# The second FFN product of an eight-batch transformer kernel, from float32 to a three-term split

## The chip, the cores and the metric

One core of one Trainium2 chip. The time is that of the device, in microseconds, of the whole program; the kernel before ran three times, the median counts.

## What is computed

An input x of 8 batches by 512 tokens by 256 features goes through a transformer of two layers, a test-time-training block, and the same transformer again:

```python
x = x + 0.5 * ffn_ref(_layernorm(x), ...)      # two layers of _layer, below
x = x + attn_ref(_layernorm(x), ...)           # TTT block, the "mid" stage
x = x + 0.5 * ffn_ref(_layernorm(x), ...)
# _layer: shift, h @ wqkv, l2norm, rotary, local attention (window 128), @ wo, residual, and then
h = layernorm(shift_token(x)) * lg + lb
a, g = split(h @ w1 + b1)                      # 256 -> 2 x 682
x = x + (a * gelu(g)) @ w2 + b2                # 682 -> 256: the product that is changed
```

The hidden width 682 is five tiles of 128 rows and a rest of 42 (`MT` = 6 tiles, `REST` = 42).

## The kernel before

Layers are numbered L = 0 to 3 (two passes of two), batches b = 0 to 7; each batch has four tiles t of 128 tokens. For each (L, b) every engine runs its own function `sequence`: four **tile stages** t = 0 to 3 (attention) and then an **FFN stage** of twelve jobs, six for each half of the batch (256 tokens). The order of the work is written out by hand, engine by engine; semaphores (`wait_ge`, `then_inc`) are the only coupling.

- **TensorE, a tile stage** (`sequence`, from line 1158): `S` (scores, in two halves, L1023), `A1` (the q, k and v products of the next tile, L963 to L965 with wqkv), `PT` (transposed probabilities, L1039), `PV` (L1053), `A0`, `A2` (transposes of k and q of the next tile, L999), `WO` (L963 to L965 with wo). At t = 2 comes `H2T` (transposed LayerNorm output of the first half). Between these stand pieces of `W2(prev, ...)`, the second FFN product of the batch **before**, cut by `cuts` into up to four fills: 12 instructions for each tile (each of the six matmuls of uT, 128 tokens, by w2, 256 columns, in float32 is recorded as two instructions at L1153).
- **TensorE, the FFN stage**: `W1` jobs 0 to 5, with `H2T` of the second half after the fifth, and jobs 6 to 11. These are 132 instructions, already split products: `split_product` (L963, L964, L965) makes upper by upper, upper by lower, lower by upper, in F32R.
- **VectorE, a tile stage**: `S` (a fused scale, mask and row minimum from PSUM, L1483), `R` (reciprocals), `A1` (eight operations of 512 columns for k and q of the next tile, L1450 to L1460, that use t1, t2 and write kqr), `O`, `A0`, `A2`, `WO` (the residual), `halves`, and `W2` (adds the second product, L1560). At t = 2 also the LayerNorm of the first half.
- **VectorE, the FFN stage**: `U` (L1553) makes uT = (a + b1) * gelu in one operation, straight from PSUM to the operand of `W2`. After the second job `LN_moments`, after the third `LN_apply` (L1544), after the fifth `H2T` (L1510).
- **ScalarE**: eight exponentials a tile stage (L733), then squares and PSUM copies; in the FFN stage twelve `G` (Gelu, L793 and L796), `H2T` after the fifth, and at the end `table(ACT.Exp)` (L783).
- **GpSimd**: `NP` (normalises the probabilities, L589), `A1` (powers and the scaling of kqr), `XB` (residual and b2 for `W2`, L596); in the FFN stage only the LayerNorm power (`LN`, L606), after which it takes the first `XB` of the next batch.

In the batches (0,0) and (2,0) there is no batch before, so their tile stages run with no `W2` at all.

Of the kernel before, what the change touches and what calls it, by code (L numbers as in the profile page):

```python
# [32 lines left out]
F32 = mybir.dt.float32  # L33
# [26 lines left out]
JOBS = (MT - 1, *range(MT - 1))  # L60


def build(nc, A):
    ctx = ExitStack()
    with ctx:
# [29 lines left out]
        w2 = sb("w2", [P, MT, D])  # L95
# [42 lines left out]
        gg = sb("gg", [P, 2, 2 * P])  # L138
        uT = sb("uT", [P, 2, MT, 2 * P])
# [5 lines left out]
        wo_s = nc.dram_tensor("wo_split", (DEPTH, P, HL * PAIRS * D), F32).ap()  # L145
        w1_s = nc.dram_tensor("w1_split", (DEPTH, P, KT * HL * W1W), F32).ap()
# [41 lines left out]
        u_done = sem("u_done", 3)  # L188
        w2_ps = sem("w2_ps", 4)
# [65 lines left out]
        m_up = [[cut(flat(sq[:, :, :], 512 * i + 256 * par, 256), NT) for par in range(2)] for i in pair]  # L255
# [32 lines left out]
        t_g, t_qd, t_a, t_m = (msems(k) for k in ("masked", "quadrant", "a_masked", "level_masked"))  # L288
        t_p_ps, t_p, t_i_ps, t_i, t_q = (msems(k) for k in ("mx_ps", "mx", "inverse_ps", "inverse", "inverse_quadrant"))
# [3 lines left out]
        s_zero = msem("hT_zero_again")  # L293
# [10 lines left out]
        def raw_piece(i):  # L304

            name, j = PIECES[i]
            if name == "wqkv":
                return cut(flat(uT[:, :, :, :], i * 1024, 1024), KT)
            if name == "wo":
                return cut(flat(w2[:, :, :], 0, PAIRS * D), PAIRS)  # L310
            return cut(flat((h, h2)[j][:, :, :], 0, 1024), KT)

        def raw_w1(j, k):
            lo, hi = W1_COLS[j]
            if j == 2:
                return flat((w2[:, 4:6, :], gg[:, :, :])[k], 0, hi - lo)
# [53 lines left out]
        def _(e):  # L370
# [27 lines left out]
            def load_rest(L):  # L398
# [58 lines left out]
            def load_out(b):  # L457
# [40 lines left out]
            def sequence(L, b, last=False):  # L498
# [50 lines left out]
            load_x(1)  # L549
# [1405 lines left out]
```

## Time and profile before

| | |
|---|---|
| median of 3 runs | 2788.74 us (2784.41 to 2792.33) |
| profiled execution | 2787.39 us, its span 2785.6 us |
| granted TensorE clock, mean | 0.995 |
| share of the span busy: PE, DVE, ACT, POOL | 98%, 75%, 59%, 48% |
| busy on L1153 (second FFN product), 1536 instructions | 435.8 us |
| chain that ended last: PE, DVE, issue, ACT | 77%, 10%, 6%, 6% |

Matmuls are pipelined, so the duration of one is longer than its distance to the next. What one costs is read from the distance between starts, in the timeline; a busy share of 98% says that something was in flight, not that the engine could take no more.

### The profile page before, as it was taken

How to read it: one execution, taken by the hardware profiler on the slowest of the kernel's cores; microseconds unless marked ns; L12 is line 12 of the kernel's file. 1: busy time of each engine (PE TensorE's matmuls, PEld its weight loads, DVE VectorE, ACT ScalarE, POOL GpSimd, SP SyncE). 2: the span in 40 equal slices, each digit the busy share in tenths (PEclk: the TensorE clock that was granted, in tenths of full speed). 3: DMA queues.
4: the chain of work that ended last, by engine and by line, in shares of the span. 5: the costliest groups of instructions: out<-in, count | busy, mean ns of one | idle time of the engine just before them, and what ended most of it. 6: DMA issues, size and time to landing. Idle time of an engine off the chain costs nothing.

```text
span 2785.6 us, 64354 instructions
## 1 busy us (share of the span) xinstructions
PE 2717.4 (98%) x22640; PEld 2316.1 (83%) x22640; DVE 2097.5 (75%) x6328; ACT 1633.0 (59%) x4358; POOL 1335.2 (48%) x1436
## 2 busy tenths in 40 slices
PE   7999999999999999998998999999999999999998
PEld 6788888888888888887766788888888888888887
DVE  7888888877777877776655778777777778777775
ACT  4656566565565666565454666656565656656564
POOL 4545555445454555543212555545454555545453
PEclk9999999999999999999999999999999999999999
DMA  2122010002000000004100000000003000000000
GB/s 103 43 77 73 24 40 28 21 28 102 13 2 2 2 2 2 2 10 172 33 26 23 2 2 2 2 2 1 2 2 111 21 2 17 17 17 17 17 17 24
DMA packets 76303, 76.47 MB, mean 27 GB/s; under 512 B 37456, under 2 KB 63312, under 8 KB 74832
## 3 DMA queue, kind: packets, MB, share of 16 engines
q1 hardware_dynamic: 70208, 70.79, 7.8%
q8 instruction: 184, 3.01, 0.5%
q10 hardware_dynamic: 5776, 1.56, 0.2%
q14 instruction: 135, 1.11, 0.1%
HBM read 47.96 MB, written 23.59 MB: 26 GB/s over the span
## 4 chain that ended last, share of the span: by engine, by line
PE 77%; DVE 10%; issue 6%; ACT 6%; POOL 1%; DMA 0%; ACTq 0%; DVEq 0%; POOLq 0%
PE bank L963 13%; PE bank L965 12%; PE bank L964 12%; PE bank L1153 11%; PE bank L1023 6%; PE bank L1053 6%; PE bank L1039 5%; ACT pr L733 4%; PE bank L999 3%; PE bank L1298 2%; DVE t L1452 2%; PE bank L1084 2%; DVE t L1455 1%; PE bank L975 1%; PE bank L1252 1%
## 5 line engine op out<-in xcount | busy, mean ns | idle before, releaser
L589 POOL TENSOR_TENSOR pr<-pr,rden 128x512 f32<-128x512 f32 (+1 forms) x512 | 469.5, 938 | 964.7 <-DVE rden L1492 960.8
L733 ACT ACTIVATE pr<-pr,nb 128x256 f32<-128x256 f32 (+1 forms) x1024 | 478.9, 469 | 273.1 <-DVE nb L1483 270.2
L1153 PE MATMUL bank<-w,uT 128*128 128x256 f32 (+1 forms) x1536 | 435.8, 399 | 0.0
L1483 DVE CUSTOM_DVE_ANT_0 pr<-bank,maskb,r 128x256 f32<-128x256 f32 (+1 forms) x1024 | 401.5, 446 | 31.5 <-PE bank L1023 20.6
L963 PE MATMUL bank<-h2T,w 128*128 128x256 f32 x1408 | 405.8, 288 | 3.9
L964 PE MATMUL bank<-h2T,w 128*128 128x256 f32 x1408 | 395.0, 281 | 0.0
L965 PE MATMUL bank<-h2T,w 128*128 128x256 f32 x1408 | 394.8, 280 | 0.0
L1553 DVE SCALAR_TENSOR_TENSOR uT<-bank,b,gg 128x256 f32<-128x256 f32 (+1 forms) x384 | 182.3, 480 | 235.4 <-ACT gg L793 141.4
L963 PE MATMUL bank<-wqkv,hT 128*128 128x512 f32 x768 | 326.9, 426 | 7.8 <-DVE nb L1483 5.8
L1153 PEld LDWEIGHTS bank<-w,uT 128*128 128x128 f32 (+1 forms) x1536 | 255.0, 189 | 59.7 <-issue 19.3
L964 PE MATMUL bank<-wqkv,hT 128*128 128x512 f32 x768 | 303.8, 396 | 0.0
L965 PE MATMUL bank<-wqkv,hT 128*128 128x512 f32 x768 | 302.5, 394 | 0.0
L793 ACT ACTIVATE gg<-bank,b 128x256 f32<-128x256 f32 x320 | 151.8, 475 | 252.7 <-PE bank L965 251.6
L744 ACT ACTIVATE pT<-bank 128x512 f32<-128x512 f32 (+1 forms) x512 | 250.8, 550 | 65.5 <-PE bank L1039 65.5
L963 PEld LDWEIGHTS bank<-h2T,w 128*128 128x128 f32 x1408 | 266.5, 189 | 20.4 <-DVE h2T L1510 10.4
L964 PEld LDWEIGHTS bank<-h2T,w 128*128 128x128 f32 x1408 | 269.3, 191 | 0.0
L1053 PE MATMUL bank<-pT,v 128*64 128x128 f32 x3584 | 262.8, 282 | 2.2 <-ACT pT L744 2.2
L965 PEld LDWEIGHTS bank<-h2T,w 128*128 128x128 f32 x1408 | 264.5, 188 | 0.0
L1023 PE MATMUL bank<-kT,qT 64*128 64x256 f32 (+1 forms) x3072 | 253.5, 293 | 2.9 <-issue 2.9
L1039 PE MATMUL bank<-ident,pr 128*128 128x128 f32 x1792 | 247.0, 277 | 5.8 <-POOL pr L589 5.8
L1053 PEld LDWEIGHTS bank<-pT,v 128*64 128x64 f32 x3584 | 200.1, 137 | 55.4 <-issue 51.5
L1039 PEld LDWEIGHTS bank<-ident,pr 128*128 128x128 f32 x1792 | 201.0, 141 | 47.2 <-issue 22.1
(226 smaller groups left out, 5932.0 us busy)
## 6 DMA issues: line engine op xcount, KB each, us to landing
wqkv<-wqkv_split SPq DMA_DIRECT2D x18, 512.0 KB, 6.5
w<-w_split SPq DMA_DIRECT2D x3, 2816.0 KB, 9.8
Y<-in_x SPq DMA_DIRECT2D x8, 512.0 KB, 7.9
out<-Y SPq DMA_DIRECT2D x8, 512.0 KB, 3.6
stt<-stt SPq DMA_DIRECT2D x224, 3.0 KB
h<-out SPq DMA_DIRECT2D x7, 512.0 KB, 3.5
out<-h SPq DMA_DIRECT2D x7, 512.0 KB, 3.0
w<-in_w SPq DMA_DIRECT2D x4, 768.0 KB, 4.8
```

The source lines that it names most:

```text
L589: e.tensor_tensor(pr[:, 2 * j:2 * j + 2, 0:wide], pr[:, 2 * j:2 * j + 2, 0:wide], rden[:, 2 * j:2 * j + 2].unsqueeze(2).to_broadcast([P, 2 ...
L733: last = e.activation(pr[:, hd, 0:wide], pr[:, hd, 0:wide], ACT.Exp, bias=nb[:, hd:hd + 1], scale=-1.0, accum_out=den[:, hd:hd + 1])
L744: e.activation(pT[:, 2 * j:2 * j + 2, 0:w, :], bank[PT_BANK[j]][:, :].rearrange("p (h w c) -> p h w c", h=2, w=2)[:, :, 0:w, :], ACT.Copy) ...
L963: e.matmul(out, left[0], right[0], start=first, stop=False)
L964: e.matmul(out, left[0], right[1], start=False, stop=False)
L965: return e.matmul(out, left[1], right[0], start=False, stop=last)
L1023: m = e.matmul(out, qT[rows, lq, p, t % 2, :], kT[rows, lk, p, slots, :], start=(i == 0), stop=(i == 2), skip_group_check=True)
L1039: mm = e.transpose(bank[bk][:, (2 * g + w) * P:(2 * g + w + 1) * P], pr[:, 2 * j + g, w * P:(w + 1) * P], ident[:, :])
L1053: mm = e.matmul(bank[6][64 * g:64 * g + 64, j * P:(j + 1) * P], v[:, tile, hd * DH:(hd + 1) * DH], pT[:, hd, w, :], start=(w == 0), stop=( ...
L1153: mm = e.matmul(bank[bk][:, 0:D], uT[0:rows, t // 2, mt, (t % 2) * P:(t % 2 + 1) * P], w2[0:rows, mt, :], start=(mt == 0), stop=(mt == MT ...
L1483: m = e.tensor_tensor_reduce(pr[:, hd, 0:wide], bank[j][:, g * 256:g * 256 + wide], far, r[:, t, 1, place(hd):place(hd) + 1], FAR, ALU.add ...
L1553: e.scalar_tensor_tensor(uT[0:rows, half, mt, :], bank[job % 4][0:rows, 0:256], b1[0:rows, L % 2, 0, mt:mt + 1], gg[0:rows, job % 2, :], A ...
```

## The change

The product a * gelu(g) by w2 is made from F32R parts. w2 is split once for each of the first two layers (upper parts by ScalarE, lower by VectorE, from the raw values, in the FFN stage of batch 0), stored to DRAM at b = 4 and loaded split in layers 2 and 3. The left operand is split in every job: VectorE writes ut, ScalarE copies it to uTh (F32R), GpSimd writes uTl = ut - uTh. For each of the five full tiles `W2` then makes three matmuls. For the rest of 42 rows the upper part lies in rows 0 to 41 of uTh and the lower part in rows 64 to 105 of the same tile (w2h holds the rest's rows twice), so two matmuls do: 17 for each tile of tokens in place of 12 instructions.

To make room, kr and qr become t1 itself (added and scaled in place, and so awaited until they are transposed), gg and ut lie in t2, qT loses its second slot, and the mid stage's buffers move (x_mid, z_T, kqT, vk, err, state, m_up, statistics).

```diff
+UNITS = 3 * (MT - 1) + 2
-        w2 = sb("w2", [P, MT, D])
+        w2h = sb("w2h", [P, MT, D], F32R)
+        m_w2l = under("raw_w2", MT * D)
+        w2l = sb("w2l", [P, MT, D], F32R)
-        kqr = sb("kqr", [P, 2, INNER])
-        kr, qr = kqr[:, 0, :], kqr[:, 1, :]
-        qT = sb("qT", [P, HL, PAIRS, 2, P], F32R)
+        kr, qr = t1[:, 0, :], t1[:, 1, :]
+        gg, ut = (t2[:, i, :].rearrange("p (a c) -> p a c", a=2) for i in range(2))
+        qT = sb("qT", [P, HL, PAIRS, P], F32R)
-        uT = sb("uT", [P, 2, MT, 2 * P])
+        uTh = sb("uTh", [P, 2, MT, 2 * P], F32R)
+        uTl = sb("uTl", [P, 2, MT - 1, 2 * P], F32R)
@@ gpsimd
+            def U_lo(L, b, half, i):
+                job, f = 6 * half + i, 8 * L + b
+                e.wait_ge(u_hi, at(u_hi, 12 * f + job + 1))
+                e.tensor_tensor(uTl[:, half, JOBS[i], :], ut[:, job % 2, :], uTh[:, half, JOBS[i], :], ALU.subtract).then_inc(u_lo, 1)
@@ gpsimd, sequence
                 LN(L, b, 1)
+                for half in range(2):
+                    for i in range(1, MT):
+                        U_lo(L, b, half, i)
@@ scalar
+            def U_hi(L, b, job):
+                half, i = divmod(job, MT)
+                mt, f = JOBS[i], 8 * L + b
+                e.wait_ge(u_done, at(u_done, 12 * f + job + 1))
+                if i == 0:
+                    e.wait_ge(w2_ps, at(w2_ps, idx(L, b, 0) + 2 * half - 2))
+                ...
+                e.activation(uTh[0:rows, half, mt, :], ut[0:rows, job % 2, :], ACT.Copy).then_inc(u_hi, 1)
@@ scalar, sequence
                 for mt in range(MT):
                     G(L, b, 0, mt)
+                    if mt:
+                        U_hi(L, b, mt - 1)
                     if mt == 4:
                         H2T(L, b, 1)
                 for mt in range(MT):
                     G(L, b, 1, mt)
+                    U_hi(L, b, MT + mt - 1)
+                    if L < DEPTH and b == 0 and 1 <= mt <= 3:
+                        split_w2_hi(L, mt - 1)
                 table(ACT.Exp)
+                U_hi(L, b, 2 * MT - 1)
@@ tensor
+                for unit in range(lo, hi):
+                    mt, i = divmod(unit, 3)
+                    if mt < MT - 1:
+                        left, right = (uTh, uTh, uTl)[i][:, half, mt, cols], (w2h, w2l, w2h)[i][:, mt, :]
+                    else:
+                        rows = (64 + REST, REST)[i]
+                        left, right = uTh[0:rows, half, mt, cols], (w2h, w2l)[i][0:rows, mt, :]
+                    mm = e.matmul(bank[bk][:, 0:D], left, right, start=(unit == 0), stop=(unit == UNITS - 1))
-                    cuts = ((0, 3, 4, 5, MT), (0, 4, 4, 5, MT), (0, 4, 4, 5, MT), (0, 3, 3, 4, MT))[t]
+                    cuts = ((0, 9, 12, 14, UNITS), (0, 11, 11, 14, UNITS), (0, 11, 11, 14, UNITS), (0, 8, 8, 11, UNITS))[t]
@@ vector
+            def U_rest(L, b, half):
+                e.wait_ge(u_hi, at(u_hi, 12 * (8 * L + b) + 6 * half + 1))
+                e.tensor_tensor(uTh[64:64 + REST, half, MT - 1, :], ut[0:REST, 0, :], uTh[0:REST, half, MT - 1, :], ALU.subtract).then_inc(u_rest, 1)
@@ vector, sequence
                     U(L, b, 0, mt)
                     if mt == 1:
                         LN_moments(L, b, 1)
+                        U_rest(L, b, 0)
                     if mt == 2:
                         LN_apply(L, b, 1)
                     if mt == 4:
                         H2T(L, b, 1)
                 for mt in range(MT):
                     U(L, b, 1, mt)
+                    if mt == 1:
+                        U_rest(L, b, 1)
+                    if L < DEPTH and b == 0 and mt > 2:
+                        split_w2_lo(L, mt - 3)
```

`U` now writes ut (two slots) and waits until the job two before it has been read by `U_hi` and `U_lo` (or `U_rest`).

## Rows read from the trace of the kernel before

**Rows 1.** Part 1 of the page: busy time, share of the span, instructions.
```profile
PE 2717.4 (98%) x22640; PEld 2316.1 (83%) x22640; DVE 2097.5 (75%) x6328; ACT 1633.0 (59%) x4358; POOL 1335.2 (48%) x1436
```
**Rows 2.** Timeline (start us, us, what, [idle before]), PE, end of the program.
```profile
2769.11 0.28 PE L965 MATMUL bank<-h2T,w 128*128 128x256 f32 x1
...
2770.52 0.28 PE L965 MATMUL bank<-h2T,w 128*128 128x256 f32 x1
2770.64 11.89 PE L1153 MATMUL bank<-w,uT 128*128 128x256 f32 x48
```
**Rows 3.** Timeline, DVE: first score operation of each stage, batch (2,5) and next.
```profile
1908.05 0.35 DVE L1483 CUSTOM_DVE_ANT_0 pr<-bank,maskb,r 128x128 f32<-128x128 f32 x1
...
1921.95 0.48 DVE L1483 CUSTOM_DVE_ANT_0 pr<-bank,maskb,r 128x256 f32<-128x256 f32 x1 [0.16 <-issue]
...
1937.26 0.48 DVE L1483 CUSTOM_DVE_ANT_0 pr<-bank,maskb,r 128x256 f32<-128x256 f32 x1 [0.16 <-issue]
...
1953.69 0.48 DVE L1483 CUSTOM_DVE_ANT_0 pr<-bank,maskb,r 128x256 f32<-128x256 f32 x1 [0.39 <-PE bank L1023]
...
1986.39 0.35 DVE L1483 CUSTOM_DVE_ANT_0 pr<-bank,maskb,r 128x128 f32<-128x128 f32 x1
```
**Rows 4.** Timeline, DVE: the same operations in batch (2,0), without W2, and next.
```profile
1519.00 0.35 DVE L1483 CUSTOM_DVE_ANT_0 pr<-bank,maskb,r 128x128 f32<-128x128 f32 x1 [2.10 <-PE bank L1023]
...
1532.37 0.48 DVE L1483 CUSTOM_DVE_ANT_0 pr<-bank,maskb,r 128x256 f32<-128x256 f32 x1
...
1546.44 0.48 DVE L1483 CUSTOM_DVE_ANT_0 pr<-bank,maskb,r 128x256 f32<-128x256 f32 x1
...
1562.43 0.48 DVE L1483 CUSTOM_DVE_ANT_0 pr<-bank,maskb,r 128x256 f32<-128x256 f32 x1 [0.66 <-issue]
...
1595.27 0.35 DVE L1483 CUSTOM_DVE_ANT_0 pr<-bank,maskb,r 128x128 f32<-128x128 f32 x1
```
**Rows 5.** Timeline, PE: fill of stage t = 1 in batch (2,5), then A1.
```profile
1922.46 1.99 PE L1153 MATMUL bank<-w,uT 128*128 128x256 f32 x8
...
1924.53 0.39 PE L964 MATMUL bank<-wqkv,hT 128*128 128x512 f32 x1
```
**Rows 6.** Timeline, ACT: a 256-column copy and its successor; last Gelu, first exponential.
```profile
1948.47 0.38 ACT L703 ACTIVATE hT<-bank 128x256 fp32r<-128x256 f32 x1
1948.78 0.60 ACT L721 ACTIVATE kT<-bank 128x512 fp32r<-128x512 f32 x1
...
1985.48 0.47 ACT L793 ACTIVATE gg<-bank,b 128x256 f32<-128x256 f32 x1 [0.94 <-PE bank L965]
...
1987.38 0.39 ACT L733 ACTIVATE pr<-pr,nb 128x128 f32<-128x128 f32 x1
```
**Rows 7.** Timeline, DVE, then PE: LayerNorm to job 6, FFN stage of (2,5).
```profile
1973.73 1.72 DVE L1544 TENSOR_SCALAR h<-Y,mv,rs 128x128 f32<-128x128 f32 x5 [0.78 <-POOL rs L606]
1975.37 0.86 DVE L1553 SCALAR_TENSOR_TENSOR uT<-bank,b,gg 128x256 f32<-128x256 f32 x2
...
1976.64 0.68 DVE L1510 TENSOR_TENSOR h2T<-bank,h2T 128x512 fp32r<-128x512 f32 x1
...
1977.38 0.39 PE L963 MATMUL bank<-h2T,w 128*128 128x256 f32 x1
```
**Rows 8.** Timeline, POOL and DVE: LN_apply alone, beside one XB, beside two.
```profile
1948.40 0.85 DVE L1544 TENSOR_SCALAR h<-Y,mv,rs 128x128 f32<-128x128 f32 x3
...
1973.61 0.74 POOL L596 TENSOR_TENSOR xb<-Y,b 128x256 f32<-128x256 f32 x1
...
1282.07 1.43 POOL L596 TENSOR_TENSOR xb<-Y,b 128x256 f32<-128x256 f32 x2
...
1282.20 2.16 DVE L1544 TENSOR_SCALAR h<-Y,mv,rs 128x128 f32<-128x128 f32 x5 [0.72 <-POOL rs L606]
```
**Rows 9.** Timeline, POOL: two powers of 128x8, stage t = 1 of (2,5).
```profile
1928.95 1.66 POOL L573 TENSOR_TENSOR r<-ssg,small 128x8 f32<-128x8 f32 x1
...
1932.10 1.99 POOL L583 TENSOR_TENSOR r<-ssg,small 128x8 f32<-128x8 f32 x1
```

More of the change, by code:

```diff
@@ L254, in build @@
         mx = [cut(m_kT[:, 1024 + 256 * i:1280 + 256 * i], NT) for i in pair]
-        m_up = [[cut(flat(sq[:, :, :], 512 * i + 256 * par, 256), NT) for par in range(2)] for i in pair]
+        m_up = [[cut(flat(t2[:, :, :], 512 * i + 256 * par, 256), NT) for par in range(2)] for i in pair]
         mid = flat(v[:, :, :], 0, 1734)
@@ L532, in sequence @@
                     store_layer0(b)
+                if L < DEPTH and b == 4:
+                    store_w2(L)
                 if L == DEPTH - 1 and last:
@@ L549, in _ @@
             load_x(1)
+            load_w2(0)
             e.wait_ge(rot_scaled, at(rot_scaled, 2))
@@ L619, in sequence @@
                 LN(L, b, 1)
-                if L == DEPTH and b == 0:
-                    for i in pair:
-                        out_rstd(B // 2 - 1, i)
+                for half in range(2):
+                    for i in range(1, MT):
+                        U_lo(L, b, half, i)
+                        if L == DEPTH and b == 0 and half and i in (3, 5):
+                            out_rstd(B // 2 - 1, i // 3 - (i == 3))
             def transformer(ps):
@@ L1022, in S @@
                             out = bank[2 * half + g][:, :].rearrange("p (h w k) -> p h w k", h=2, w=2)[:, s_, slots, :]
-                            m = e.matmul(out, qT[rows, lq, p, t % 2, :], kT[rows, lk, p, slots, :], start=(i == 0), stop=(i == 2), skip_group_check=True)
+                            m = e.matmul(out, qT[rows, lq, p, :], kT[rows, lk, p, slots, :], start=(i == 0), stop=(i == 2), skip_group_check=True)
                             if s_ == 1 and i == 2:
@@ L1142, in W2 @@
                 n = idx(L, b, t)
+                f, half = 8 * L + b, t // 2
                 if L == 0 and t == 0 and lo == 0:
@@ L1145, in W2 @@
                 if lo == 0:
[L1146 to L1148 removed]
+                    if t == 0 and L < DEPTH:
+                        e.wait_ge(w2_lo, at(w2_lo, 3 * (L + 1)))
+                    elif t == 0:
+                        e.wait_ge(w2_loaded, at(w2_loaded, 32 * L))
+                    e.wait_ge(u_hi, at(u_hi, 12 * f + 6 * half + 6))
+                    e.wait_ge(u_lo, at(u_lo, 10 * f + 5 * half + 5))
+                    e.wait_ge(u_rest, at(u_rest, 2 * f + half + 1))
                     if bk == 7:
                         e.wait_ge(xf_done, at(xf_done, n))
[L1151 to L1155 removed]
+                cols = slice((t % 2) * P, (t % 2 + 1) * P)
+                for unit in range(lo, hi):
+                    mt, i = divmod(unit, 3)
+                    if mt < MT - 1:
+                        left, right = (uTh, uTh, uTl)[i][:, half, mt, cols], (w2h, w2l, w2h)[i][:, mt, :]
+                    else:
+                        rows = (64 + REST, REST)[i]
+                        left, right = uTh[0:rows, half, mt, cols], (w2h, w2l)[i][0:rows, mt, :]
+                    mm = e.matmul(bank[bk][:, 0:D], left, right, start=(unit == 0), stop=(unit == UNITS - 1))
+                if hi == UNITS:
                     mm.then_inc(w2_ps, 1)
@@ L1920, in layouts @@
     out["w2"][:, :HID] = g["L0_ffn_w2"]
+    out["w2"][:, full + 64:full + 64 + REST] = g["L0_ffn_w2"][:, full:]
     sw = np.r_[DH // 2:DH, 0:DH // 2]
```

125 lines of the change are left out of this document (74 added, 51 removed).

## The prediction, made before the changed kernel was built or run

> **What bounds the kernel now.** The page says TensorE 98% [rows 1], but matmuls overlap, so I read distances between starts. The timeline of TensorE at the end of the program gives both prices of the change: from 2769.11 to 2770.52 lie twelve F32R matmuls of 256 columns, 1.41 / 12 = 0.118 us each, and the 48 float32 instructions behind them take 11.89 us, 0.248 each [rows 2]. By these prices the second product costs 12 x 0.248 = 2.97 us for each tile of tokens.
>
> Then the timeline of VectorE, stage by stage. The distances of the first score operations in a usual batch are 13.90, 15.31, 16.43 and 32.70 us (the last holds t = 3 and the FFN stage), 78.34 in all [rows 3]. The profile holds the experiment that matters most: batch (2,0) has no product before it, so its stages run with none of the 11.9 us that the others give to L1153, and they take 13.37, 14.07, 15.99 and 32.84 us, 76.27 in all [rows 4]. Taking **all** of the second product away saves 2.07 us a batch, not 11.9. The kernel is not bound by TensorE alone: a loop through VectorE, ScalarE and GpSimd (scores, exponentials, A1, the split copies, residual) is nearly as long. Only t = 1 is clearly TensorE's, with 1.24 us to gain; t = 0 has 0.53, t = 2 has 0.44, and t = 3 with the FFN stage has none. With 30 batches that have such product in their stages, 30 x 2.07 = 62 us (2.2%) is the most that relief of TensorE can bring, whatever it saves in itself.
>
> **What the change takes from TensorE.** 17 units of 0.118 us are 2.01 us in place of 2.97, so 0.96 for each tile, 128 times, 123 us of the engine's time [rows 2]. What of it counts, stage by stage:
>
> - t = 1. The first fill goes from 8 instructions to 11 units. Before, it took from 1922.46 to the second A1 matmul at 1924.53 less one matmul of 512 columns (0.23), 1.84 us [rows 5]; after, 11 x 0.118 = 1.30, so 0.54 less. The piece between the transposes stays as it is (two instructions, 0.50, less overlap, against three units, 0.35, with two changes of form around it): I take 0. The last goes from 0.50 to 0.35. Sum 0.69. The other loop allows 14.07 plus what the product needs there even if it is short (0.35 of last fill ahead of the next scores), 14.42 [rows 4]; TensorE gives 15.31 - 0.69 = 14.62 [rows 3]. The later counts: gain **0.70**. Bounds 0.4 to 1.24.
> - t = 2. VectorE has the first half's LayerNorm in its way and is the later one. Only the last fill, 0.15, stands ahead of the scores it waits for: gain **0.15**, bounds 0 to 0.44 [rows 3, 4].
> - t = 3, up to the output projection. VectorE again; I take 0.12, bounds 0 to 0.3. What the fill after the projection saves (0.28) goes into a wait: the second H2T of the FFN stage waits for LayerNorm, whose chain starts at the residual, not at TensorE. Rows 4 show it: the stage pair is 32.84 without any fill.
> - t = 0. Here something is added. Before the first exponential stand now two copies: `U_hi` of job 10 behind the last Gelu, and, behind the table load, `U_hi` of job 11. A copy of 256 columns holds ScalarE 0.31 us (1948.47 to 1948.78, out of PSUM; from SBUF no row) [rows 6], so the exponential that started 1.90 us after the last Gelu (1985.48 to 1987.38) starts 0.62 later. A1 of VectorE hangs on the end of the exponentials. The floor is 13.37 without the product; with the last fill (0.35) and the copies (0.62) 14.34, of which I take off 0.14 since the stage of rows 4 has a wait for a slower TensorE in it. 14.20 against 13.90: **0.30 lost**, bounds 0 to 0.6.
>
> Together 0.70 + 0.15 + 0.12 - 0.30 = 0.67 us gained a batch, 30 batches, **20.1 us**.
>
> **What it adds in the FFN stage.** ScalarE: 12 copies of 0.31; VectorE: two `U_rest`; GpSimd: ten `U_lo` of 128x256 at the price of an `XB`, the same shape with two SBUF operands, 0.74 [rows 8]. One job of W1 lasts 12 x 0.118 = 1.41 us, and Gelu (0.47) and copy fill 0.8 of it, so the rate holds. But the chain through LayerNorm is what TensorE waits for: LN_apply, U(3), H2T on ScalarE, H2T on VectorE at 1976.64, and job 6 at 1977.38, right at its end [rows 7]. Three things lengthen it.
>
> - `U_hi(3)` stands before H2T on ScalarE and waits for U(3), which comes after LN_apply on VectorE (1975.37, done about 1975.80). H2T's copies then start one copy later: **0.31** [rows 6, 7]. Bounds 0.2 to 0.4.
> - LN_apply gets GpSimd beside it. Alone it takes 0.85 / 3 = 0.28 an operation, 1.42 for five; beside one XB 1.72 [rows 7, 8]; beside two 2.16 [rows 8]. Today GpSimd takes one XB there; after, `U_lo` of jobs 1 and 2 are both ready when the LayerNorm power is done, and the XB comes behind all ten. So two, and **0.44** more, in all but (1,7) and (3,7), which have two XB there already. Bounds 0 to 0.74.
> - `U_rest(0)` comes on VectorE just as GpSimd starts the LayerNorm power. A power beside an addition of two SBUF operands took 1.99, not 1.66 [rows 9]: 0.33 for an operation twice as wide. I take **0.10**, bounds 0 to 0.33.
>
> Sum 0.85 a batch, 32 batches, less 2 x 0.44: **26.3 us lost**.
>
> Here the Trainium skill speaks against the change. Its page "SBUF — State Buffer", section "SBUF: two separate sides", says that VectorE and GpSimd share a port pair that is an exclusive lock held for a whole instruction. By that rule the operations of LN_apply could stand still for two whole `U_lo`, some 1.4 us, where the rows show 2.16 - 1.42 = 0.74 for the two.
>
> **The rest.** The last four W2 run free: 4 x 0.96 = 3.9 us off the end [rows 2]; VectorE and the stores behind it are as before. The mid stage starts behind `XB`, which now waits for `U_lo` of job 11, behind the table load: my estimate, from 1.28 of load, 0.31 and 2 x 0.74, is 2 us later, bounds -3.9 to +3. Splitting w2: one of its subtractions of 512 columns (about 0.6; 0.68 at 1976.64 [rows 7]) stands right before the scores in (0,1) and (1,1): 1.2. The in-place kr and qr add waits for transposes one tile back, long done; behind those waits would stand all of VectorE's A1. The extra loads and stores of w2 (SP's queue, 768 KB each) have a stage or more to land: 0, and 5 us a time if that cover is gone. `U` waiting for `U_lo` two jobs back has about 0.3 us to spare: 0.
>
> **Sum.** -20.1 + 26.3 - 3.9 + 2.0 + 1.2 = +5.5. The profiled execution took 2787.4, so 2792.9; the median is 1.3 above it: **2794 us**.
>
> **The rivals.** (a) GpSimd beside LN_apply costs nothing new and the copies fit into waits: the FFN stage loses only 0.31. Then 9.9 us in place of 26.3: 2778, faster by 0.4%. For it: one XB was there before, too, and operations could just take turns. Against it: batches (1,7) and (3,7), 2.16 against 1.72. With t = 1 and t = 2 at their bounds it reaches 2765. Chance 0.27. (b) The lock decides: `U_lo` not only lengthens LN_apply by a part but stops it, 1.1 more than now in place of 0.44, in 30 batches; 2794 + 20 = 2814, slower by 0.9%. By the page's rule named above this would be the outcome. It decides from the point at which the FFN stage grows by more than 0.95 us a batch. For it: GpSimd is in use in the FFN stage ten times as much. Against it: 2.16 is measured with two in a row. With milder forms (0.3 more by waits of `U` for `U_lo`, 10 us) chance 0.36 for everything above +0.3%. (c) The change does what TensorE's share promises, 123 us, 2665: rows 4 speak against it; 0.01, counted with (a). My own case, within 0.3% (8.4 us, about what a measurement of this kernel can tell), 0.37: it is a balance of two sums of 20 and 26 us, and each can be off by a third.
>
> So faster 0.27, same 0.37, slower 0.36. The range takes in (a) without its bounds and most of (b): 2768 to 2814.
>
> **What would show it.** TensorE's fills at 0.118 a unit; stage t = 1 at 14.6 us, t = 2 at 16.3, t = 0 at 14.2; LN_apply at about 2.2 us and job 6 starting 0.85 us later after the residual of t = 3; first exponential 2.5 us after the last Gelu; the run of free W2 at the end 3.9 us shorter. It is wrong if t = 0 is not longer, if LN_apply stays at 1.7, or if t = 1 stays above 15.

## The result: slower by 1.15%, just outside the range

The changed kernel took 2819.52 us (median of 4 runs, 2817.96 to 2823.89) against 2787.77 for the kernel before (four runs now); the ratio is 1.0115, 95% interval 1.0097 to 1.0134. Forecast was 2794 with a range up to 2814, so the outcome that I held likeliest (no change) did not come, and 26 us are to be explained. The profiled execution took 2823.9 us, its span 2822.1; it is the slowest of the four, so what single batches show in it can be more than the median has.

Part 1 of the page of the changed kernel (busy time, share of the span, instructions), which answers to [rows 1]:
```profile
PE 2690.0 (95%) x23280; PEld 2319.4 (82%) x23280; DVE 2146.8 (76%) x6398; ACT 1757.2 (62%) x4748; POOL 1577.9 (56%) x1758
```
TensorE lost 27 us of busy time, the three others gained 49, 124 and 243 with the copies and subtractions. The timeline of VectorE, first score operation of each stage of batch (2,5) and of the next batch, answers to [rows 3]:
```profile
1938.08 0.35 DVE L1550 CUSTOM_DVE_ANT_0 pr<-bank,maskb,r 128x128 f32<-128x128 f32 x1
...
1952.40 0.48 DVE L1550 CUSTOM_DVE_ANT_0 pr<-bank,maskb,r 128x256 f32<-128x256 f32 x1
...
1967.20 0.48 DVE L1550 CUSTOM_DVE_ANT_0 pr<-bank,maskb,r 128x256 f32<-128x256 f32 x1
...
1983.60 0.48 DVE L1550 CUSTOM_DVE_ANT_0 pr<-bank,maskb,r 128x256 f32<-128x256 f32 x1 [0.38 <-PE bank L1078]
...
2017.13 0.35 DVE L1550 CUSTOM_DVE_ANT_0 pr<-bank,maskb,r 128x128 f32<-128x128 f32 x1
```
The distances are 14.32, 14.80, 16.40 and 33.53 us, 79.05 in all. Against [rows 3]:

| stage | before | after | change | forecast |
|---|---|---|---|---|
| t = 0 | 13.90 | 14.32 | +0.42 | +0.30 |
| t = 1 | 15.31 | 14.80 | -0.51 | -0.70 |
| t = 2 | 16.43 | 16.40 | -0.03 | -0.15 |
| t = 3 and FFN | 32.70 | 33.53 | +0.83 | +0.73 |
| batch | 78.34 | 79.05 | +0.71 | +0.18 |

Every step has its forecast sign, and every one came out on the dear side: 0.53 us in this batch, 16 us if all 30 are like it (added up through the whole trace it is 14). The rest is in a few stages, most of which I had costed at next to nothing.

The FFN stage is the largest loss of (2,5). Timelines of DVE, POOL and ACT, changed kernel, answering to [rows 7, 8]:
```profile
1996.98 0.42 DVE L1570 TENSOR_TENSOR Y<-bank,Y 128x256 f32<-128x256 f32 x1
...
2003.75 2.15 DVE L1611 TENSOR_SCALAR h<-Y,mv,rs 128x128 f32<-128x128 f32 x5 [0.51 <-POOL rs L624]
...
2007.40 0.68 DVE L1577 TENSOR_TENSOR h2T<-bank,h2T 128x512 fp32r<-128x512 f32 x1
...
2002.26 1.40 POOL L624 TENSOR_TENSOR rs<-vare,small 128x5 f32<-128x5 f32 x1 [5.87 <-DVE vare L1599]
2003.62 1.42 POOL L634 TENSOR_TENSOR uTl<-t,uTh 128x256 fp32r<-128x256 f32 x2
...
2006.33 0.42 ACT L842 ACTIVATE uTh<-t 128x256 fp32r<-128x256 f32 x1 [1.40 <-DVE t L1625]
...
2006.70 0.59 ACT L813 ACTIVATE h2T<-bank 128x512 fp32r<-128x512 f32 x1
```
and two rows of the same timelines of the kernel before that did not stand ahead:
```profile
1967.15 0.42 DVE L1503 TENSOR_TENSOR Y<-bank,Y 128x256 f32<-128x256 f32 x1
...
1972.47 1.17 POOL L606 TENSOR_TENSOR rs<-vare,small 128x5 f32<-128x5 f32 x1 [6.00 <-DVE vare L1532]
```
From the residual to H2T on VectorE: 1976.64 - 1967.15 = 9.49 us before, 2007.40 - 1996.98 = 10.42 after. LN_apply, beside two `U_lo`, takes 2.15 for 1.72; the power of LayerNorm, beside `U_rest`, 1.40 for 1.17; and `U_hi(3)` stands ahead of H2T.

### The profile page after: what moved, and what is told of

It is laid out like the page before. It is cut to its first block, busy times and chain, and to the rows that moved or that the text cites. A ratio compares the mean times of both kernels' runs of the same rounds, so it can differ in the third digit from the quotient of the medians.

```text
span 2822.1 us, 66713 instructions
## 1 busy us (share of the span) xinstructions
PE 2690.0 (95%) x23280; PEld 2319.4 (82%) x23280; DVE 2146.8 (76%) x6398; ACT 1757.2 (62%) x4748; POOL 1577.9 (56%) x1758
## 4 chain that ended last, share of the span: by engine, by line
PE 52%; DVE 19%; ACT 12%; issue 8%; POOL 7%; ACTq 2%; DMA 1%; DVEq 0%; POOLq 0%
PE bank L1018 9%; PE bank L1020 8%; PE bank L1019 8%; ACT pr L767 7%; PE bank L1219 5%; PE bank L1108 4%; PE bank L1078 4%; PE bank L1094 3%; PE bank L1054 3%; DVE t L1523 3%; DVE t L1520 3%; PE bank L1363 2%; POOL pr L607 2%; DVE pr L1550 2%; DVE h L1611 2%
## 5 line engine op out<-in xcount | busy, mean ns | idle before, releaser
L634 POOL TENSOR_TENSOR uTl<-t,uTh 128x256 fp32r<-128x256 f32 x320 | 238.1, 748 | 277.3 <-ACT uTh L842 277.3
L1625 DVE SCALAR_TENSOR_TENSOR t<-bank,b,t 128x256 f32<-128x256 f32 (+1 forms) x384 | 181.8, 480 | 215.5 <-ACT t L830 102.2
L1018 PE MATMUL bank<-wqkv,hT 128*128 128x512 f32 x768 | 306.2, 399 | 8.5 <-DVE nb L1550 5.7
L1019 PE MATMUL bank<-wqkv,hT 128*128 128x512 f32 x768 | 305.5, 398 | 0.0
L1020 PE MATMUL bank<-wqkv,hT 128*128 128x512 f32 x768 | 302.5, 394 | 0.0
L827 ACT ACTIVATE t<-bank,b 128x256 f32<-128x256 f32 x320 | 151.5, 474 | 149.6 <-PE bank L1020 145.2
L1219 PE MATMUL bank<-w2h,uTh 128*128 128x256 f32 (+1 forms) x768 | 237.7, 310 | 2.9 <-issue 1.5
L1078 PE MATMUL bank<-kT,qT 64*128 64x256 f32 (+1 forms) x3072 | 232.9, 286 | 3.8 <-issue 2.9
```

The costliest lines, as they stand in the source:

```text
L634: e.tensor_tensor(uTl[:, half, JOBS[i], :], ut[:, job % 2, :], uTh[:, half, JOBS[i], :], ALU.subtract).then_inc(u_lo, 1)
L1018: e.matmul(out, left[0], right[0], start=first, stop=False)
L1019: e.matmul(out, left[0], right[1], start=False, stop=False)
L1020: return e.matmul(out, left[1], right[0], start=False, stop=last)
L1078: m = e.matmul(out, qT[rows, lq, p, :], kT[rows, lk, p, slots, :], start=(i == 0), stop=(i == 2), skip_group_check=True)
L1219: mm = e.matmul(bank[bk][:, 0:D], left, right, start=(unit == 0), stop=(unit == UNITS - 1))
```

## The experiments

Each starts from the changed kernel unless said otherwise; ratios are to the kernel before, on the same chip.

**pe_only: TensorE's part alone.**
```diff
-    e.scalar_tensor_tensor(ut[0:rows, job % 2, :], ...)
+    e.scalar_tensor_tensor(uTh[0:rows, half, mt, :], ...)
-    left, right = (uTh, uTh, uTl)[i][:, half, mt, cols], (w2h, w2l, w2h)[i][:, mt, :]
+    left, right = uTh[:, half, mt, cols], (w2h, w2l, w2h)[i][:, mt, :]
-    U_hi(...)    U_lo(...)    U_rest(...)
```


> The changed kernel with its TensorE part alone: VectorE's U writes the activation straight into the first half tile, all 17 units read that as left operand, and the lower part of the activation, with U_hi, U_lo and U_rest on ScalarE, GpSimd and VectorE, is left out of the computation. The split of w2 stays, with its copies and loads. My theory (the saving on TensorE is real but mostly in stages that another loop bounds): t = 1 stays at about 14.8 us as in the changed kernel, t = 0 goes from 14.35 back to 13.9 or below, FFN stage with t = 3 from 33.5 back to about 32.6, so about 77.5 us a batch against 78.35 before; 30 x 0.85 = 25 us gained, less some 10 us that stay in single batches, where w2 is split and stored: 2765 to 2778, and never the 123 us. Rival 1 (TensorE bounds every stage, the helper work eats the rest): 2665. Rival 2 (the loss of the changed kernel lies in the new matmul program itself, in its changes of kind and row configuration): still over 2790.

2764.47 us, 0.9915 (0.990 to 0.993). Batch (2,5): 13.61, 14.80, 16.42, 32.53. So the new matmul program, with the split and the store of w2 still in it, is worth 24 us, not 123, and the helper work with its waits costs 55. Rival 2 falls: t = 1 is the same 14.80 with and without the helper work, t = 0 and the FFN stage are not.

**before_one: the kernel before with one of its six second-product matmuls.**
```diff
-    for mt in range(lo, hi):
+    for mt in range(MT - 1, hi):
```


> The kernel before with five of the six matmuls of each second product left out (the short one stays, two instructions of 0.25 us a tile), everything else as it was. It tests the bound that was read from the batch without such a product: 30 batches x at most 2.07 us less the remaining last fill ahead of the scores, so 40 to 60 us in the stages, and 4 x 2.47 = 10 us at the end: 2720 to 2740. Rival (TensorE's share of 98% is what bounds the time): 128 x 2.47 = 316 us less, 2472.

2746.81 us, 0.9859 (0.9845 to 0.9874): 316 us of TensorE's work gone, 39 us of time. In (2,5): 13.63, 14.48, 16.48, 32.54. The bound read from the single batch of [rows 4] holds, but my range for this run (2720 to 2740) does not: 1.2 us a batch were gained of the 2.07. t = 2 gained nothing, for its last fill is the short matmul that this kernel keeps.

**act_h2t: ScalarE's H2T ahead of `U_hi(3)`.**
```diff
     G(L, b, 0, mt)
+    if mt == 4:
+        H2T(L, b, 1)
     if mt:
         U_hi(L, b, mt - 1)
-    if mt == 4:
-        H2T(L, b, 1)
```


> One place of the changed kernel: on ScalarE the second H2T of the FFN stage goes ahead of the upper copy of job 3 again. My theory (this copy stands in the chain residual, LayerNorm, H2T, job 6): the gap of TensorE ahead of that H2T shrinks by 0.3 to 0.4 us, the FFN stage by 0.31, so 10 to 12 us in 32 batches, about 2808. Rival (VectorE's part of the chain is the later one, since LN_apply beside GpSimd and U of job 3 come first): the gap stays, under 3 us, 2817 to 2820.

2809.59 us, 1.0076 (1.0061 to 1.0092). The FFN stage goes from 33.53 to 33.22, by the 0.31 of one copy; 10 us in all. The copy was in the chain.

**pool_ln: GpSimd off VectorE's side during LN_apply.**
```diff
     LN(L, b, 1)
+    e.wait_ge(h2n_done, at(h2n_done, 9 * b + (72 * L + 9)))
```


> One wait added in the changed kernel: GpSimd starts the ten U_lo of a batch only when LN_apply of the second half is done. This takes GpSimd off VectorE's side during LN_apply. Theory A (the two lengthen each other by a part): LN_apply's five operations go from 2.15 to 1.42 us; but the U_lo, and with them U of jobs 2 to 4 that wait for them, come 2 us later, and XB at the end of the stage too. If U has that much to spare, 0.7 us a batch are gained, 22 us, about 2798; if not, the gain is given back at job 4 or at the end of the stage and the time stays within 5 us of 2819. Theory B (the slow LN_apply has another cause than GpSimd's subtractions, such as XB or waits within it): LN_apply stays above 2 us and the time gets longer by what the U_lo lose.

2828.39 us, 1.0144 (1.0129 to 1.016), 9 us slower than the changed kernel. Timelines of DVE, POOL and ACT in (2,5) of pool_ln:
```profile
2002.15 0.42 DVE L1571 TENSOR_TENSOR Y<-bank,Y 128x256 f32<-128x256 f32 x1
...
2008.92 1.37 DVE L1612 TENSOR_SCALAR h<-Y,mv,rs 128x128 f32<-128x128 f32 x5 [0.51 <-POOL rs L624]
2011.23 0.48 DVE L1626 SCALAR_TENSOR_TENSOR t<-bank,b,t 128x256 f32<-128x256 f32 x1 [0.94 <-POOL uTl L634]
...
2012.82 0.68 DVE L1578 TENSOR_TENSOR h2T<-bank,h2T 128x512 fp32r<-128x512 f32 x1
...
2010.36 1.43 POOL L634 TENSOR_TENSOR uTl<-t,uTh 128x256 fp32r<-128x256 f32 x2 [1.54 <-DVE h L1612]
...
2011.75 0.42 ACT L843 ACTIVATE uTh<-t 128x256 fp32r<-128x256 f32 x1 [1.65 <-DVE t L1626]
```
LN_apply takes 1.37 us alone, so two `U_lo` cost it 0.78: theory B falls. How they do it stands in the rows of the changed kernel, one operation at a time (narrow windows of the timelines of POOL and DVE):
```profile
2003.62 0.74 POOL L634 TENSOR_TENSOR uTl<-t,uTh 128x256 fp32r<-128x256 f32 x1
2003.75 0.70 DVE L1611 TENSOR_SCALAR h<-Y,mv,rs 128x128 f32<-128x128 f32 x1 [0.51 <-POOL rs L624]
2004.32 0.73 POOL L634 TENSOR_TENSOR uTl<-t,uTh 128x256 fp32r<-128x256 f32 x1
2004.37 0.76 DVE L1611 TENSOR_SCALAR h<-Y,mv,rs 128x128 f32<-128x128 f32 x1
2005.05 0.34 DVE L1611 TENSOR_SCALAR h<-Y,mv,rs 128x128 f32<-128x128 f32 x1
```
An operation of LN_apply that starts beside a `U_lo` gives way to the next one only when the `U_lo` ends (2003.62 + 0.74, then 2004.32 + 0.73). It is so in all 64 such pairs of this trace: the next one starts 3 to 10 ns after that end. So VectorE got through one operation for each `U_lo`. The two `U_lo` last 1.42 us; 0.13 of it had passed when LN_apply began, and two operations of 0.26 are done within it, which leaves the loss of 0.78. But U(3) now waits 0.94 for the first `U_lo`, `U_hi(3)` for U(3), and H2T stands behind `U_hi(3)`: 10.67 from residual to H2T instead of 10.42. The gain turned into a wait. Theory A had named that wait of `U` for `U_lo`, but not that H2T hangs on it, and its "within 5 us of 2819" missed.

**ln_clear: the chain taken out of that order.** act_h2t, pool_ln, and VectorE's H2T behind U(3):
```diff
-    if mt == 4:
+    if mt == 3:
         H2T(L, b, 1)
```


> Three moves in the changed kernel: ScalarE's H2T ahead of the upper copy of job 3; GpSimd's ten U_lo only behind LN_apply; VectorE's H2T behind U of job 3 instead of job 4. The second alone made the kernel 9 us longer, though LN_apply went from 2.15 to 1.37 us. Theory A (that gain was given back through U of job 3, which waits for the first U_lo, and ScalarE's copy behind it, ahead of H2T): with H2T taken out of that order on both engines the 0.78 us count, FFN stage about 32.5 to 32.7 against 33.2 with the first move alone, 2819 - 10 - 15 = about 2794. Theory B (the later U_lo hold up U of jobs 3 and 4 and so W1 of jobs 6 and 7 for as long): FFN stage 33.1 or above, 2806 or more.

2793.42 us, 1.0025 (1.0016 to 1.0034); 26 us, as much as the FFN stages had lost. The same view of ln_clear, DVE:
```profile
1978.06 0.42 DVE L1571 TENSOR_TENSOR Y<-bank,Y 128x256 f32<-128x256 f32 x1
...
1984.83 1.37 DVE L1612 TENSOR_SCALAR h<-Y,mv,rs 128x128 f32<-128x128 f32 x5 [0.51 <-POOL rs L624]
1987.15 0.48 DVE L1626 SCALAR_TENSOR_TENSOR t<-bank,b,t 128x256 f32<-128x256 f32 x1 [0.95 <-POOL uTl L634]
...
1987.61 0.68 DVE L1578 TENSOR_TENSOR h2T<-bank,h2T 128x512 fp32r<-128x512 f32 x1
```
9.55 us from residual to H2T, as before the change (9.49), with the same 0.95 of waiting in U(3): it is no longer ahead of H2T on ScalarE. The stage takes 32.66, 0.87 less than in the changed kernel: the 0.31 of the copy and 0.56 of the 0.78. pool_ln alone does not bring the second part. VectorE's own move of H2T was not run by itself, so its share is not known.

**oneoffs: two places that come up in single batches.**
```diff
+    stats_moved(L, b)
     store_w2(L)                    # b == 4
-    if L < DEPTH and b == 0 and mt > 2:
-        split_w2_lo(L, mt - 3)
+    if L < DEPTH and b == 0 and 2 <= mt <= 4:
+        split_w2_lo(L, mt - 2)
```


> Two places of the changed kernel that come up in a few batches only: the store of the next layer's split w2 is issued behind the transfers of the LayerNorm sums of batch 4 instead of ahead of them, and the two splits of w2's lower part on VectorE go from behind jobs 3 and 4 to behind jobs 2 and 3. Theory (the store's 1.5 MB stand in the way of small transfers on which LayerNorm waits; the split makes TensorE wait 1.4 us and its clock fall to 1.2 GHz for some 7 us): batch (1,4) from 37.85 back to about 33.5 us in its last stage, t = 0 of (0,1) and (1,1) from 17.05 to about 14.5 if the splits fit there; together 4 + 5 = 9 us, about 2810. Rival (the store has the queues full for as long wherever it stands, and the split has no room before the scores): the stalls move to the next stage and less than 3 us are gained.

2811.37 us, 1.0081 (1.0064 to 1.0098). First the store, changed kernel, batch (1,4); SP's and VectorE's timelines:
```profile
1058.59 0.65 SPq L380 DMA_DIRECT2D stt<-stt  x1
1059.28 0.53 SPq L428 DMA_DIRECT2D w_split<-w2h  x1
1059.86 0.58 SPq L428 DMA_DIRECT2D w_split<-w2l  x1
...
1065.78 0.28 DVE L1592 BATCH_NORM_AGGREGATE mv<-stt 128x2 f32<-128x12 f32 x2 [3.02 <-DMA stt<-stt]
```
LayerNorm's sums, 3 KB, are in flight together with the 2 x 768 KB of the store, which is issued 0.7 us behind the first of them, and VectorE waits 3.02 us for them. With the store behind these transfers the last stage of (1,4) goes from 37.85 to 33.55. The loss is there in every run that keeps the old order (37.2 to 38.5). Then the splits, batch (1,1), timelines of VectorE and TensorE and the busy times by window (PE, PEld, DVE, ACT, POOL, granted clock) of the changed kernel:
```profile
757.71 1.08 DVE L1635 TENSOR_TENSOR w2l<-raw_w,w2h 128x512 fp32r<-128x512 f32 x1
...
758.85 0.39 PE L1219 MATMUL bank<-w2h,uTh 128*128 128x256 f32 x1 [1.41 <-DVE w2l L1635]
```
```profile
760.00:762.00 2.00, 2.00 (x15) 1.88 (x14) 1.01 (x8) 1.36 (x8) 0.98 (x3) 0.50 0.03 8
762.00:764.00 2.00, 2.00 (x7) 1.65 (x7) 0.63 (x5) 1.31 (x8) 1.98 (x4) 0.50 0.00 0
```
The last split holds VectorE 1.08 us and TensorE's second product waits 1.41 us for it; behind that wait the granted clock is 0.50, TensorE's 1.2 GHz level, from 760 to 766 (two of the three windows stand here), and the stage takes 17.03 instead of 14.33. One job earlier, in oneoffs, the stage takes 14.19 and the clock stays at 1.00; in (0,1) it is 17.05 and 14.71.

But this is not the gain of the move. The other runs that leave the splits where they were have this wait too (1.1 us in copy_first, 1.4 in the others) and not always the fall. Batch (1,1) of ln_clear, TensorE, and its windows:
```profile
750.83 0.39 PE L1220 MATMUL bank<-w2h,uTh 128*128 128x256 f32 x1 [1.40 <-DVE w2l L1636]
...
751.00:753.00 2.00, 2.00 (x21) 1.79 (x22) 1.56 (x14) 1.90 (x10) 1.42 (x2) 1.00 0.03 8
```
There the clock stays at 1.00, in the windows that follow too, and the stage takes 13.96. Over the eight traces with the old order (the changed kernel, act_h2t, pool_ln, ln_clear, copy_first, rest_rows, cuts, cut_t2) this stage takes 13.96 to 17.03 in (1,1) and 14.14 to 17.06 in (0,1); the two together take 29.7 to 34.1, against 28.9 in oneoffs, by how far and how long the clock falls. rest_rows and act_h2t, which do not touch the splits, have 14.14 in (0,1). What is steady is one stage earlier: the last stage of (1,0), in which the splits stand, takes 34.4 to 35.0 us in all of these but ln_clear and 33.8 in oneoffs, and 33.9 in ln_clear against 32.9 in best3: 1.0 us for the move. So of the 8.2 us that oneoffs gained by the medians, 4.3 are the store and 1.0 are steady gain of the splits; the other 2.9 agree with a clock that falls in some executions, and are not shown.

**copy_first: ScalarE's last two copies moved.** `U_hi` of job 10 ahead of the last Gelu, that of job 11 behind the exponentials of the first score group:
```diff
+    if mt == MT - 1:
+        U_hi(L, b, MT + mt - 1)
     G(L, b, 1, mt)
...
     S(L, b, t, j)
+    if t == 0 and j == 0 and prev:
+        U_hi(*prev, 2 * MT - 1)
```


> The changed kernel with two copies of ScalarE moved: the upper copy of job 10 goes ahead of the last Gelu (into the 0.63 us in which ScalarE waits for W1), that of job 11 behind the exponentials of the first score group. Nothing is left out. My theory (before the first exponential of a batch stand two copies that were not there, and A1 hangs on the exponentials): the first exponential comes 0.6 to 0.8 us earlier, t = 0 goes from 14.35 to about 13.75, 30 x 0.6 = 18 us, about 2801; the FFN stage keeps 33.5. Rival (the lower copy of job 11 and with it XB and the four multiplications of GpSimd become the later loop, since they now start behind the moved copy): t = 0 stays at 14.2 or above, under 5 us gained.

2812.34 us, 1.0091 (1.0075 to 1.0108). Both theories miss: t = 0 goes to 14.08, not 13.75, and not 14.2 or above. The first exponential does start early enough (ACT's timeline of copy_first; the score operations start at 1932.38):
```profile
1931.47 0.47 ACT L827 ACTIVATE t<-bank,b 128x256 f32<-128x256 f32 x1
...
1933.36 0.39 ACT L767 ACTIVATE pr<-pr,nb 128x128 f32<-128x128 f32 x1
...
1934.13 0.40 ACT L842 ACTIVATE uTh<-t 128x256 fp32r<-128x256 f32 x1
1934.44 0.39 ACT L767 ACTIVATE pr<-pr,nb 128x128 f32<-128x128 f32 x1
```
but the eight exponentials and the squares behind them run without a gap on ScalarE, so a copy among them costs its 0.31. A start is not the chain: I had moved one copy out of it and the other only along it.

**rest_rows: both rest units on 106 rows.**
```diff
-    rows = (64 + REST, REST)[i]
+    rows = 64 + REST
```


> The changed kernel with both matmuls of the short last contraction on 106 rows, in place of one on 106 and one on 42; that adds the product of the two lower parts for those 42 rows. My theory (a change of the row count between two matmuls costs TensorE about 0.1 us, 0.21 in place of 0.12 in the trace): stage t = 1, which TensorE bounds, from 14.80 to 14.70, the others unchanged; 30 x 0.1 = 3 us, 2813 to 2819. Rival (the longer distance behind that matmul belongs to the change of kind, not of rows): no change of t = 1, within 1 us.

2817.37 us, 1.0111 (1.0096 to 1.0126), not told apart from the changed kernel; t = 1 stays at 14.83. The theory was wrong for that stage. But the free run at the end shows the price. Starts of the last two residuals on VectorE, changed kernel, then rest_rows (before, they start at 2779.58 and 2782.57):
```profile
2816.63 0.42 DVE L1641 TENSOR_TENSOR Y<-bank,xb 128x256 f32<-128x256 f32 x1 [0.97 <-PE bank L1219]
...
2819.02 0.42 DVE L1641 TENSOR_TENSOR Y<-bank,xb 128x256 f32<-128x256 f32 x1 [1.51 <-PE bank L1219]
```
```profile
2809.09 0.42 DVE L1641 TENSOR_TENSOR Y<-bank,xb 128x256 f32<-128x256 f32 x1
...
2811.10 0.42 DVE L1641 TENSOR_TENSOR Y<-bank,xb 128x256 f32<-128x256 f32 x1 [1.13 <-PE bank L1219]
```
A tile takes 2.99 us before, 2.39 and 2.01 in these two. 2.01 is 17 x 0.118, as forecast; the single matmul of 42 rows adds 0.38. TensorE's own starts say the same: it does not take the 0.38 itself, but three distances around it grow, 0.21 from the 106-row matmul to it, 0.31 behind it and 0.22 behind the one after, in place of 0.12 each.

**cuts and cut_t2: the last three units moved to the first fill**, in t = 1 and t = 2, and in t = 2 alone.
```diff
-    (0, 11, 11, 14, UNITS), (0, 11, 11, 14, UNITS)      # t = 1, t = 2
+    (0, 14, 14, UNITS, UNITS), (0, 14, 14, UNITS, UNITS)  # cuts
+    (0, 11, 11, 14, UNITS), (0, 14, 14, UNITS, UNITS)     # cut_t2
```


> That move of the last three units of t = 1 and t = 2 alone, in the changed kernel. It tests why t = 1 got 0.51 us shorter and not the 0.70 expected. Theory (fragments: a piece of three units of 0.118 costs 0.45 and not 0.35): t = 1 from 14.80 to 14.65, t = 2 within 0.05 of 16.41, 3 to 5 us less than 2819.5. Rival (what is left in t = 1 is no change of kind): t = 1 stays within 0.03 of 14.80, time the same.

> The changed kernel with the last three units of the second product moved from behind the output projection to the first fill in t = 2 alone. Done in t = 1 and t = 2 together it made t = 1 longer by 0.38 us and t = 2 shorter by 0.37. Theory A (in t = 1 these units are covered by four VectorE operations ahead of the scores, while the first fill is on the path; in t = 2 it is the other way round, there VectorE waits for the last fill and the score matmuls behind it): t = 2 from 16.41 to 16.04, t = 1 stays at 14.80, 30 x 0.37 = 11 us less, 2808. Theory B (t = 2 only gave back what t = 1 had lost, by a chain that runs over both): t = 2 stays within 0.05 of 16.41, no gain.

cuts: 2819.52 us, 1.0114 (1.0099 to 1.0129); t = 1 is 15.18, t = 2 is 16.04. Neither theory came true; the time is the same as the rival said, but only since 0.38 lost and 0.36 gained cancel. cut_t2: 2809.33 us, 1.0078 (1.0063 to 1.0093), with 14.81 and 16.01 in (2,5): its theory A. The rows say why. In t = 1 of the changed kernel VectorE goes from the residual through four operations straight into the scores:
```profile
1965.83 0.42 DVE L1570 TENSOR_TENSOR Y<-bank,Y 128x256 f32<-128x256 f32 x1 [0.23 <-PE bank L1020]
...
1967.20 0.48 DVE L1550 CUSTOM_DVE_ANT_0 pr<-bank,maskb,r 128x256 f32<-128x256 f32 x1
```
so the last fill is covered there and the first one is on the path; in t = 2 the score row at 1983.60 has waited 0.38 for L1078, the scores behind the last fill.

**best3, best4, best6: the moves together.** best3 is ln_clear, oneoffs and copy_first. best4 has the copy of job 11 on GpSimd instead, and drops the wait on `u_hi` in A1 that the one on `u_lo` implies. best6 is best4 with cut_t2.
```diff
+    if job == 2 * MT - 1:
+        e.tensor_copy(uTh[:, half, JOBS[i], :], ut[:, job % 2, :])   # GpSimd
```


> All moves that gained by themselves in the changed kernel, together: the three of the LayerNorm chain, the store and the splits of w2, the two moved copies of ScalarE. If the terms are independent: 2819.5 less 26 less 8 less 7 = 2778, faster than the kernel before by 0.3%; per batch 14.07, 14.80, 16.40, 32.65. If one took its gain from the other (the same wait counted twice), 2785 to 2795.

> As the other, but the upper copy of job 11 is made by GpSimd, which is idle at that point, right behind U, and one of the two waits at the head of A1 of t = 1 (the one that the other implies) is dropped. With the copy behind the first score group, 0.3 us of it still stood in ScalarE's chain of exponentials and squares: t = 0 went to 14.07, not to 13.75. Theory: without it and one wait t = 0 goes to 13.65 to 13.75, 30 x 0.35 = 10 us less, about 2768. Rival (copy and subtraction of GpSimd take 1.4 us beside VectorE's score operations and lengthen these, or XB comes too late): t = 0 at 14 or above, 2778.

> The fastest version so far (2763.3 us, per batch 13.65, 14.80, 16.39, 32.63) with that move in t = 2. Theory A: 16.04 in t = 2, 11 us less, 2752, 1.3% under the kernel before. Theory B: 2763. If the three units are also the cover of something in the FFN stage, that gets longer than 32.7.

2777.38 us, 0.9963 (0.995 to 0.9976); 2763.28 us, 0.9911 (0.9895 to 0.9928); **2752.59 us, 0.9871 (0.9854 to 0.9887)**, which beats both kernels. The stages of (2,5) in best6, first score operations on VectorE:
```profile
1889.22 0.35 DVE L1557 CUSTOM_DVE_ANT_0 pr<-bank,maskb,r 128x128 f32<-128x128 f32 x1
...
1902.82 0.48 DVE L1557 CUSTOM_DVE_ANT_0 pr<-bank,maskb,r 128x256 f32<-128x256 f32 x1
...
1917.62 0.48 DVE L1557 CUSTOM_DVE_ANT_0 pr<-bank,maskb,r 128x256 f32<-128x256 f32 x1
...
1933.67 0.48 DVE L1557 CUSTOM_DVE_ANT_0 pr<-bank,maskb,r 128x256 f32<-128x256 f32 x1 [0.34 <-issue]
...
1966.28 0.35 DVE L1557 CUSTOM_DVE_ANT_0 pr<-bank,maskb,r 128x128 f32<-128x128 f32 x1
```
13.60, 14.80, 16.05 and 32.61: 1.28 less than before in a batch, with all the work of the change in it. Most of the loss lay in the order and place of the helper work, not in its amount: best4, which does all of it, takes as long as pe_only, which leaves it out (2763.28 and 2764.47), though best4 has at least 4 us from the moved store that pe_only does not have. Not all of the lead over the kernel before is due to the change, though: the move of cut_t2, worth 11 us, takes TensorE's work out of a place where it was in the kernel before too, and that kernel was not run with it. (best5, best4 with the move of cuts in both stages, took 2765.11 us, 0.9919: what t = 2 gained t = 1 lost.)

## Why the prediction missed, step by step

Two kinds of step failed. TensorE's saving a tile was mis-sized, and costs of single places were put at nothing or near it with no row behind them: the waits ahead of A1, the store of w2, the splits of w2. The main mechanism was right.

- **Rows 4 as the bound: right.** pe_only and before_one give 24 and 39 us where the engine's own work fell by 77 (0.60 a tile, next point) and 316; 62 was the most by rows 4.
- **0.96 us saved a tile: wrong.** It is 0.60 (2.99 less 2.39). I costed the 42-row unit like the others. The first fill of t = 1, without that unit, took 1.39 instead of 1.30 (0.23 for its first unit), so 0.45 gained instead of 0.54; the free run at the end got 12.0 - 9.6 = 2.4 shorter, not 3.9.
- **t = 1, 0.70: the last fill's 0.15 does not count there.** VectorE's four operations cover it (cuts). Measured 0.51.
- **t = 2, 0.15: right place, wrong size.** The last fill is on that path. With none the stage takes 16.00 to 16.05 (cut_t2, and (2,0) before and after), so the two float32 instructions cost 0.43 and not 0.50, the three units 0.37 and not 0.35: 0.03 gained by the rows of (2,5).
- **t = 0, 0.30: mechanism right, 0.12 short.** The first exponential starts 2.50 us after the last Gelu, as forecast. Beyond the copies stand the waits at A1 that I had put at 0. Idle time ahead of its first operation, in stages t = 0 and t = 1 of the changed kernel (the A1 of the second has neither wait), then in t = 0 of best4 with one of the two:
```profile
1943.53 0.69 DVE L1518 TENSOR_REDUCE ssk<-sq 128x8 f32<-128x512 f32 x1 [0.48 <-ACT sq L743]
...
1957.90 0.69 DVE L1518 TENSOR_REDUCE ssk<-sq 128x8 f32<-128x512 f32 x1 [0.31 <-ACT sq L743]
```
```profile
1902.60 0.69 DVE L1525 TENSOR_REDUCE ssk<-sq 128x8 f32<-128x512 f32 x1 [0.37 <-ACT sq L749]
```
  Both semaphores had been raised 3 us before; two waits cost 0.17, one 0.06. The medians of the 24 batches of layers 1 to 3 are the same 0.48, 0.31 and 0.37, and pe_only, which has neither wait, has 0.32 in t = 0. In (0,2) to (0,6) the stage grew by 0.64 to 0.74, more than the 0.42 here; no run took that apart.
- **FFN stage, 0.85: right to 0.1.** `U_hi(3)` 0.31 (act_h2t 0.31), LN_apply 2.15 (forecast 2.16; alone it takes 1.37, which I had read as 1.42), the power beside `U_rest` 0.23 where I took 0.10 (0.19 of it reached the chain): chain 0.93 longer. Rival (b) forecast 1.1 more for LN_apply than before and 0.43 came. Its sum was wrong, not the rule beneath it. By the Trainium skill's page "SBUF — State Buffer", section "SBUF: two separate sides", an operation of VectorE that needs the port pair shared with GpSimd and finds it taken waits for GpSimd's whole instruction. The trace agrees as to the wait: 64 of 64 operations of LN_apply that began beside a `U_lo` made way only at its end (pool_ln, above). What I had added up to 1.4 us is 0.78, for part of the first `U_lo` had passed, and a held operation takes no time of its own behind the release.
- **The mid stage, +2: open.** My terms (1.28, 0.31 and 2 x 0.74) add up to 3.1, and the prediction does not say why 2 was taken. The stage of (1,7) that holds it grew by 1.89, where 2.3 were forecast with its FFN part, but it varies from 256.9 to 260.8 us over the runs that keep the rest of the changed kernel, so the agreement proves little.
- **Single batches, 1.2 us and 0: wrong.** I named "5 us a time if that cover is gone" for the extra DMAs, a figure with no row behind it, and took 0. In (1,4) the cover was gone, and it cost 4.3 us. The splits cost 1.08 each beside `U_lo`, not 0.6 (0.68 in pe_only, which has no `U_lo`), and TensorE waits 1.4 us for the last. With the clock at 1.00 behind that wait, the 0.6 us for (1,1) would have been about right (in ln_clear the last stage of (1,0) is 1.2 longer than its neighbours and the stage behind it 0.4 shorter); with the clock at 0.50, as in the profiled execution, t = 0 of (0,1) and (1,1) took 4.9 us more together than their neighbours.

**The sum.** The spans of the two profiled executions differ by 36.5 us where 5.5 were forecast, so the trace has 31 us to place, five more than the medians. Added up by stages against the forecast: 14 in the usual ones, 4.4 in (1,4), 4.3 in t = 0 of (0,1) and (1,1), 5.0 in the last stages of (0,0), (1,0), (2,0) and (2,1), 1.2 in that of (3,3), where VectorE waited 0.98 us for LayerNorm's sums, and 2.7 in (3,7) and the end, of which the free run is 1.5. What stays open: the last stages of (2,0) and (2,1) take 34.5 to 34.7 us in the changed kernel and still 33.8 in best6, against 32.6 in the usual batches of best6; no run took these apart. Nor did one hold the clock, so how often it falls behind the splits is not known.

## What to carry to other kernels

List, for each helper operation that a change adds, which instruction stands right behind it on its engine and whether the loop runs through that one: nearly all of the 55 us of loss here hung on the place of a few of them, and a copy off by one position cost its full length. When two losses share a chain, removing one alone can show a loss (pool_ln, 9 us) though both together bring 26; try the order as a whole. And look up the one batch in which a big store meets a small transfer that somebody waits for. Before a stage of one trace is called a gain, look at the same stage in every other run that left it alone: here it varied by 3 us with the clock.

## What the runs showed of the hardware

- VectorE's tensor_scalar of 128x128 beside a GpSimd subtraction of 128x256 does not get slower by a share; it is let go when the subtraction ends, 3 to 10 ns later in 64 of 64 cases. Beside two of them, five take 2.15 us and not 1.37.
- A wait of TensorE of 1.4 us is followed by a granted clock of 0.50 in some executions and of 1.00 in others, with the same instructions around it; with the fall the stage takes 15.5 to 17.1 us in place of 14.0 to 14.3.
- A matmul of 42 rows among ones of 128 costs 0.38 us beyond its 0.118 (2.39 against 2.01 a tile). Ahead of scores on 64 rows it costs less: in t = 2 of the changed kernel they follow it by 0.01 us, where they follow a matmul of 106 rows by 0.21 (rest_rows), so t = 2 is the same in both.
- Two waits on semaphores raised 3 us before cost VectorE 0.17 us.
- GpSimd's plain copy of 128x256 takes 0.40 us, as long as ScalarE's row (0.41), while its subtraction of the same shape takes 0.73 (timeline of POOL, best4):
```profile
1898.02 0.40 POOL L637 CAST uTh<-t 128x256 fp32r<-128x256 f32 x1 [0.20 <-DVE t L1632]
1898.50 0.73 POOL L639 TENSOR_TENSOR uTl<-t,uTh 128x256 fp32r<-128x256 f32 x1
```
